# Latent attention of a two-layer decoder: the last probability tile of each batch is turned on TensorE instead of by transfers

## The reference

```python
xn = _layernorm(x, gamma_media, beta_media)          # the 1024 context tokens
ln = _layernorm(latents, gamma_lat, beta_lat)        # the 512 tokens of the batch
q = ln @ Wq + bq
kv_input = jnp.concatenate([xn, ln], axis=1)         # 1536 keys
kv = kv_input @ Wkv + bkv
k, v = jnp.split(kv, 2, axis=-1)                     # 8 heads of 128
q = q * DH ** (-0.5)
sim = jnp.einsum('bhid,bhjd->bhij', q, k)
attn = jax.nn.softmax(sim, axis=-1)
out = jnp.einsum('bhij,bhjd->bhid', attn, v)
out = out.transpose(0, 2, 1, 3).reshape(b, -1, INNER)
return out @ Wo + bo
```

## Time and profile before

| | us |
|---|---|
| median of 3 runs | 2011.17 |
| lowest and highest run | 2007.79, 2012.63 |
| the profiled execution's own time | 2012.13 |
| its span | 2010.3 |
| TensorE matmuls busy | 1825.7 (91%) |
| VectorE busy | 1621.6 (81%) |
| ScalarE busy | 1277.7 (64%) |

### The profile page before, as it was taken

How to read it: one execution, slowest core, us unless ns; L and a number is a source line. 1 busy time by engine, 2 the same in 40 slices (tenths; PEclk the granted TensorE clock), 3 DMA queues, 4 the chain that set the end, 5 groups by cost and what they waited for, 6 DMA issues and landing times.

```text
span 2010.3 us, 41782 instructions
## 1 busy us (share of the span) xinstructions
PE 1825.7 (91%) x17100; PEld 1024.9 (51%) x17100; DVE 1621.6 (81%) x2631; ACT 1277.7 (64%) x1915; POOL 239.7 (12%) x250
## 2 busy tenths in 40 slices
PE   4999988989999997989999998898999999898977
PEld 3677753322567773232557775332257776323235
DVE  8888878698778878789688887869788887868954
ACT  6666645669566655738756664556856664574852
POOL 1000001120300001030210000112030000103513
PEclk8999999999999999999999999999999999999988
DMA  7366630010166660001056663001035666000225
GB/s 314 85 127 128 128 90 13 5 32 23 48 129 127 127 126 30 6 16 41 12 112 127 127 134 69 13 9 28 23 67 127 127 121 137 9 6 22 88 65 123
DMA packets 448653, 157.82 MB, mean 79 GB/s; under 512 B 426149, under 2 KB 439728, under 8 KB 447952
## 3 DMA queue, kind: packets, MB, share of 16 engines
q1 hardware_dynamic: 442768, 145.68, 32.7%
q0 software_dynamic: 2384, 6.36, 1.0%
q10 hardware_dynamic: 3312, 3.11, 0.6%
HBM read 33.96 MB, written 9.47 MB: 22 GB/s over the span
## 4 chain that ended last, share of the span: by engine, by line
PE 58%; DVE 29%; ACT 5%; DMA 4%; issue 4%; POOL 0%; ACTq 0%; POOLq 0%; DVEq 0%
DVE nmx L2316 15%; PE ps L796 9%; PE ps L798 9%; PE ps L797 9%; PE ps L1186 6%; PE ps L970 4%; PE ps L1172 4%; PE ps L964 3%; PE ps L965 3%; DMA arena<-arena 3%; PE ps L1136 1%; DVE arena L2120 1%; DVE st L1941 1%; PE ps L1196 1%; PE ps L1253 1%
## 5 line engine op out<-in xcount | busy, mean ns | idle before, releaser
L2316 DVE TENSOR_REDUCE nmx<-ps 128x2 f32<-128x1024 f32 x384 | 444.8, 1218 | 16.1 <-PE ps L1136 14.6
L1761 ACT ACTIVATE arena<-ps 128x512 f32<-128x512 f32 x768 | 406.9, 600 | 53.2 <-PE ps L1172 48.8
L2105 DVE TENSOR_SCALAR_CACHE_REDUCE ps<-ps 128x1536 f32<-128x1536 f32 x128 | 225.7, 1763 | 37.7 <-PE ps L798 37.1
L1186 PE MATMUL ps<-arena 128*17 128x256 f32 x3072 | 242.2, 391 | 0.0
L2120 DVE SCALAR_TENSOR_TENSOR arena<-arena,rs 128x1536 f16<-128x1536 f32 x128 | 231.6, 1809 | 4.2 <-ACT arena L1651 4.2
L1651 ACT ACTIVATE arena<-arena,rs 128x1536 f16<-128x1536 f32 x128 | 200.8, 1569 | 42.9 <-DVE rs L2111 42.9
L1642 ACT ACTIVATE arena<-ps,nm 128x1536 f32<-128x1536 f32 x128 | 197.1, 1540 | 9.6 <-DVE ps L2105 9.6
L964 PE MATMUL ps<-arena 128*128 128x128 f16 x1536 | 185.3, 219 | 0.9 <-DMA arena<-arena 0.9
L965 PE MATMUL ps<-arena 128*128 128x128 f16 x1536 | 185.3, 219 | 0.0
L796 PE MATMUL ps<-arena 128*128 128x512 f16 (+2 forms) x508 | 174.3, 347 | 6.9 <-DMA arena<-zx_d 5.3
L798 PE MATMUL ps<-arena 128*128 128x512 f16 (+2 forms) x508 | 174.3, 347 | 0.0
(11 more groups left out here) (356 smaller groups left out, 3506.3 us busy)
## 6 DMA issues: line engine op xcount, KB each, us to landing
arena<-in_weights SPq DMA_DIRECT2D x8, 929.0 KB, 22.4
arena<-arena SPq DMA_DIRECT2D x72, 64.0 KB, 2.1
arena<-arena SPq DMA_TRANSPOSE x268, 3.2
arena<-in_ctx SPq DMA_DIRECT2D x4, 1024.0 KB, 5.3
arena<-in_ctx_t SPq DMA_DIRECT2D x4, 1024.0 KB, 4.9
arena<-in_experts SPq DMA_DIRECT2D x1, 3840.0 KB, 11.5
arena<-zx_d ACTq DMA_DIRECT2D x23, 132.0 KB, 2.5
arena<-arena SPq DMA_DIRECT2D x72, 32.0 KB, 1.9
```

What stands on the lines that cost most here:

```text
L1186: mm(ps[32 * j:32 * j + VW, 7, cols], v17[:, kt, 4 * g_ + j, :], pr_[:, (4 * t + j) % RING, cols], start=(kt + half == 0), stop=(kt == mod ...
L1761: A(pr_[:, n % RING, :], ps[:, 4 + n % 3, :], ACT.Exp).then_inc(b_exp.sem, 1)
L2105: TS_(s_, s_, -XS, None, ALU.mult, ALU.min, accum_out=nm[:, i:i + 1]).then_inc(s_max.sem, 1)
L2316: V.tensor_reduce(nmx[:, g_ % 2, ch, :, pp, i], ps[:, 2 * (z % 2):2 * (z % 2) + 2, :], AX.X, ALU.max, negate=True)\
```

## The change

In each batch the last tile's two DMA transposes go. In their place:

- TensorE turns the high part's 12 blocks (`turn_last(0)`) between the high and the low matmuls of tile 2: eight into bank 3, four into bank 4. ScalarE copies both banks to `xpT[1][0]`.
- TensorE turns the low part's 12 blocks (`turn_last(1)`) after `late(range(2))`: eight into bank 5, and, once the high part's copies have been made, four into bank 4. ScalarE copies bank 5 and VectorE bank 4 to `xpT[1][1]`.
- Each copy raises `th_in[1]` or `tl_in[1]` by 8, where a transfer raised it by 16, so that the waits in `weighted` stay as they are.
- VectorE's copy stands after the bias and ahead of both halves of the last head's output. ScalarE's three copies stand ahead of `last_output_hi`.

```diff
-        o_mm, o_q, o_hi, o_lo = sig("o_mm", NTI), sig("o_q", XH + 1), sig("o_hi", XH + 1), sig("o_lo", XH + 1)
+        o_mm, o_q, o_hi, o_lo = sig("o_mm", NTI + 4), sig("o_q", XH + 1), sig("o_hi", XH + 1), sig("o_lo", XH + 1)
...
-                for it in range(NTI // 2 - 1):
-                    for s_ in range(2):
-                        transpose_hi(b, 2 * it + 2 + s_, s_, True)
-                        transpose_lo(b, 2 * it + 2 + s_, s_)
+                for n in range(2, NTI - 1):
+                    transpose_hi(b, n, n % 2, True)
+                    transpose_lo(b, n, n % 2)
...
+                def turn_last(part):
+
+                    done = (s_hi, s_lo)[part]
+                    pe.wait_ge(done.sem, done.at(b, NTI))
+                    for bank, kts in ((3 + 2 * part, range(8)), (4, range(8, KT_TILES))):
+                        if part and bank == 4:
+                            pe.wait_ge(th_in[1].sem, th_in[1].at(b, 16 * (NTI // 2)))
+                        for k, kt in enumerate(kts):
+                            last = nc.tensor.transpose(ps[:, bank, :].bitcast(F16)[:, P * k:P * k + P], xq[1][part][:, P * kt:P * kt + P],
+                                                       ident16[:])
+                        last.then_inc(o_mm.sem, 1)
...
-                weighted(b, 2, h, par, bank=2)
+                weighted(b, 2, h, par, lambda: turn_last(0), bank=2)
                 late(range(2))
+                turn_last(1)
                 weighted(b, 3, h, par, lambda: late(range(2, 4)), bank=2)
...
                 for k in range(2):
+                    act.wait_ge(o_mm.sem, o_mm.at(b, NTI - 1 + k))
+                    A(xpT[1][0][:, 8 * k:8 * k + 8 - 4 * k, :].rearrange("p a n -> p (a n)"),
+                      ps[:, 3 + k, :].bitcast(F16)[:, 0:P * (8 - 4 * k)], ACT.Copy).then_inc(th_in[1].sem, 8)
+                act.wait_ge(o_mm.sem, o_mm.at(b, NTI + 2))
+                A(xpT[1][1][:, 0:8, :].rearrange("p a n -> p (a n)"), ps[:, 5, :].bitcast(F16), ACT.Copy).then_inc(tl_in[1].sem, 8)
+                for k in range(2):
                     last_output_hi(b, k)
...
-                dve.wait_ge(o_mm.sem, o_mm.at(b, NT * (XH - 1) + 2 * k + 2))
+                dve.wait_ge(o_mm.sem, o_mm.at(b, NTI + 4 if k else NTI - 2))
...
                 add_rows("xbo")
+                dve.wait_ge(o_mm.sem, o_mm.at(b, NTI + 3))
+                V.tensor_copy(xpT[1][1][:, 8:KT_TILES, :].rearrange("p a n -> p (a n)"), ps[:, 4, :].bitcast(F16)[:, 0:P * 4])\
+                    .then_inc(tl_in[1].sem, 8)
                 last_output_full(b, 0)
```

## The result

| | before | after |
|---|---|---|
| median of 10 runs, us | 2011.03 | 2016.34 |
| lowest and highest | 2007.79, 2016.38 | 2013.88, 2021.77 |
| span of the profiled execution | 2010.3 | 2016.1 |

The ratio is 1.0022, 95% interval 1.0012 to 1.0031: slower by 4.4 us (5.3 by the medians), inside the 0.3% that was called no change, though the interval's upper end just passes it. The forecast was 2014.8.

What follows compares the result with a forecast made beforehand. TensorE was taken to bound the end of the latent stage; the four batches' 1.34 + 1.34 + 0.67 + 0.29 = +3.6 us on the median 2011.17 gave 2014.8 us, own range 2013 to 2017, overall 2010.5 to 2019.5.

Steps and rivals of the forecast that it cites:

- The turns: TensorE, last tile of each batch: 24 turns at 0.056 us, 1.34 us a batch, 5.4 us in all, on the path.
- The copies: ScalarE and VectorE copies of turned blocks: 0 us, hidden under TensorE's work, with 0.8 and 1.6 us in hand.
- The waits: TensorE's waits for transfers at the batches' ends: 1.54 us in batch 2, 0.88 in batch 3 within tiles 2 to 3.
- the wait of batch 2: TensorE's 1.54 us ahead of tile 2's low part: 0.67 us of turns run inside it, so only +0.67 counts.
- batch 3 gain by the transfer that was gone: No transfer to wait for at tile 3's high part: 7.98 us in place of 7.69, +0.29.
- the cause: Instruction-queue packets of 16 KB, one per about 250 TensorE instructions, delay transposes beside them; waits of 0 to 1.5 us each.
- Faster: Whole program faster by 6 us, more than all waits at the batches' ends together (5.03 us); chance 0.05.
- Waits vanish: Rival: moved packets fall where no tile waits in batches 1 to 3; +1.6 us, 2012.8 us; chance 0.18.
- Waits grow: Rival: two more transposes held up where TensorE feels it, 1.4 us each, up to 2020 us; chance 0.10.
- The clock falls: Rival: TensorE granted half its clock in the turns at each batch's end; +10.2 us, 2021.4 us; chance 0.10.
- A copy is late: Rival: ScalarE's high copies miss 269.43 and TensorE waits up to 1 us a batch; +7.6 us; chance 0.03.

Runs made afterwards that it cites:

- one part alone: Changed kernel with only the last tile's high part turned on TensorE, the low part transposed by DMA again: 2012.91 us, ratio 1.0010 to the kernel before.
- twice the turns: Changed kernel with every block turned twice into the same place, 48 turns a batch for 24: 2025.2 us, ratio 1.0063 to the kernel before.
- The shifts: Both kernels with 32 or 64 one-column matmuls added in batch 0: 64 places, before 1.0000, changed 1.0056; 128 places, before 0.9995, changed 1.0010.
- one wait filled: Both kernels with projections of heads 0 to 5 between tile 1's high and low matmuls, last head: before 2009.71 us (0.9997), changed 2009.55 (0.9991).

## Why the prediction was right

**The turns.** Right to the hundredth: 0.056 us each, 0.67 for 12, 1.34 a batch, no cover; one part alone gives 7.31, twice the turns 9.32. The 0.390 us of the Trainium skill ("VectorE: DVE Perf Modes", the three transpose paths) is seven times what stands here, where turns follow each other.

**The copies.** Right: nothing waits for them. ScalarE's two high copies take 1.51 us where 1.62 were reckoned, VectorE's 0.42, below the 0.48 to 0.69 that the nearest rows gave.

**The waits.** Here a step of the sum failed. It let the wait of batch 2 stay where it was, with half of the turns inside it (+0.67 for the batch, a window of 9.02), and batch 3 gain by the transfer that was gone (+0.29). Both waits had moved ahead of tile 1, where neither turns nor the missing transfers reach them, and they measured 2.04 and 1.25 us; batch 1's grew from 1.33 to 1.63. So the turns counted in full, 5.4, and the waits rose by 1.2: +6.6 at the batches' ends in place of +3.6. Outside them 0.8 came back in the profiled execution; what did that was not traced, and the forecast had no such term.

The prediction had named the cause and said that the packets would come earlier, to transfers of tile 1, while the sum was still made with the old places. The shifts bear the cause out. By them the change costs 0.0022, 0.0056 and 0.0015 of the time at no shift, 64 and 128 places (after's ratio less that of the kernel before with the same shift), 0.0031 in the mean, 6.2 us, beside 5.4 for the turns. That the two lie so close is partly luck: the 0.0056 holds three meetings of packet and scatter in the changed kernel, the 0.0015 one such meeting in the kernel before, and with one wait filled the change cost nothing. The range held because it left room for waits that move; that the forecast itself came within 2 us is in part luck with where they went.

One reading of the trace was also off. The other tiles were said to pass nearly without a wait. Before the change TensorE waits 1.1 to 1.4 us for head 6's tile 3 in every batch, and 1.4 to 1.8 us in the first head of batches 1 to 3, beside the scatter. *Faster* was thus judged against 5.0 us of waits where the program has 15.2 for these transfers.

**The rivals.** *Waits vanish*: not here; with 128 places' shift they nearly did in the changed kernel's last heads, and its time was still 1.0010. *Waits grow*: in part, +1.2. *The clock falls* in the turns: no, 1.00 in all four windows and with twice the turns. The Trainium skill's statement ("TensorE: Matmul & The Clock Gate", Part 4) that transposes don't count as TensorE being busy for the full clock shows no effect here, with 12 and with 24 turns in a row between dense matmuls; no run has more of them in a row. *A copy is late*: no.

## What to carry to other kernels

A transfer that has landed before its reader comes costs the reader nothing, so doing its work on the bounding engine costs that work in full. Look first for the waits that do stand on the path. Moving independent work over them took the changed kernel from 1.0022 to 0.9991 and 0.9972, but the kernel before gained nothing by it, because its next transfers were then late, and at another placement the changed kernel gained nothing either (1.0010 and 1.0011). A difference of a few tenths of a per cent should be tested at several placements of the instruction stream before it is put down to the edit, since here the placement alone moved the changed kernel between 1.0010 and 1.0056 of the kernel before.

## What the runs showed of the hardware

The instruction queue's packets of 16 KB go with TensorE's instructions: 137 packets for 34392 of them, and from one packet to the next TensorE starts 180 to 326 in the kernel before, 258 in the middle (those of its sequencer included). A 1536x128 transpose landed after 3.2 us in the middle where no packet and no scatter ran beside it. What a packet does to it depends on when it comes. In the 14 traces, scatters left out, the middle was 3.2 us again when the packet began up to 1 us ahead of the issue, 3.7 when it began within 0.5 us behind it, and 4.8 (4.2 to 5.9) when it began 1 to 2 us behind it. I had expected a packet to cost up to 1.5 us in a wait; 2.04 was seen beside one, and 3.0 to 3.9 where a scatter was under way too, with a fall of the clock behind five of those eight waits.
